# Two-layer graph network on one core: where VectorE's addition to the logits of four groups stands in the first edge pass

## The reference, cut to what matters

```python
msg_s = (s_n @ Ws_src)[src] + (s_n @ Ws_dst)[dst]          # and the same for the vectors
m1_s, m1_v = _cg_tp(msg_s, msg_v, y0, y1, w1[...])         # products with the harmonics y and weights rbf @ W_rbf
a = (m1_s @ W_alpha).reshape(e, H, AS_)
a = jnp.where(a > 0, a, 0.2 * a)
a = jnp.sum(a * alpha_dot, axis=-1, keepdims=True)         # the logits: 4 heads for each edge
val_s = m1_s @ Ws_val
val_v = jnp.einsum('ecx,cd->edx', m1_v, Wv_val) * jax.nn.sigmoid(val_s @ Wg)[..., None]
m2_s, m2_v = _cg_tp(jax.nn.sigmoid(val_s), val_v, y0, y1, w2_ss, ...)
h = ...                                                    # m2 @ Ws_vlin and Wv_vlin, weighted by softmax(a) later
```

## Time and profile before

| what | value |
|---|---|
| time, median of 3 runs | 9161.6 us (9114.4 to 9190.4) |
| profiled execution: device time | 9135.8 us |
| profiled execution: span of the instructions | 9134.0 us |
| TensorE busy | 7569 us (83%) |
| VectorE busy | 6767 us (74%) |
| ScalarE busy | 5161 us (57%) |
| mean granted TensorE clock | 0.86 |
| VectorE's additions to the logits | 98, 22.2 us busy, 254.2 us idle before them |

### The profile page before, as it was taken

One profiled execution on the slowest core, in us unless ns is written; L12 is line 12 of the kernel. 1 busy time (PEld: TensorE's weight loads), 2 busy tenths in 40 slices (PEclk: granted clock), 3 DMA queues, 4 the chain that ended last, 5 costly groups with the idle time before them and its releaser, 6 DMA issues. The chain is left out here.

```text
span 9134.0 us, 197714 instructions
## 1 busy us (share of the span) xinstructions
PE 7569.2 (83%) x43972; PEld 5972.6 (65%) x43973; DVE 6766.6 (74%) x16742; ACT 5161.1 (57%) x16950; POOL 5109.3 (56%) x5222
## 2 busy tenths in 40 slices
PE   5788888888888888888888886997778888888788
PEld 3677777777777777777777776995444444444446
DVE  7777777777777777777777787887667767767677
ACT  5555555555555555555555552116666666667675
POOL 0556666555555555655655555870666655566650
PEclk7788888888788788888888797998899989999999
DMA  7333333223222232322332234766444434444345
GB/s 251 79 83 87 85 85 84 79 83 85 79 83 83 79 85 83 84 83 81 84 83 83 82 80 150 236 204 112 107 110 111 112 106 110 111 109 114 108 110 180
DMA packets 971877, 968.06 MB, mean 106 GB/s; under 512 B 452750, under 2 KB 788750, under 8 KB 971662
## 3 DMA queue, kind: packets, MB, share of 16 engines
q0 software_dynamic: 225792, 385.65, 17.1%
q1 hardware_dynamic: 512032, 346.40, 13.8%
q10 hardware_dynamic: 233936, 234.90, 7.7%
HBM read 677.57 MB, written 288.65 MB: 106 GB/s over the span
## 5 line engine op out<-in xcount | busy, mean ns | idle before, releaser
L754 POOL DMA_INDIRECT e_g_dst<-table_dst,e_idx x1568 | 1518.9, 969 | 1159.5 <-issue 622.8
L754 POOL DMA_INDIRECT e_g_src<-table_src,e_idx x1568 | 1560.9, 995 | 996.6 <-issue 803.3
L2028 POOL DMA_INDIRECT f_e<-table,f_src x1568 | 1494.0, 953 | 980.1 <-issue 530.3
L793 PE MATMUL e_ps_t<-ident,e_m 128*128 128x128 f32 (+1 forms) x7840 | 1405.9, 331 | 471.1 <-issue 193.2
L793 PEld LDWEIGHTS e_ps_t<-ident,e_m 128*128 128x128 f32 (+1 forms) x7840 | 1121.6, 168 | 618.4 <-issue 365.8
L2085 PE MATMUL f_ps_a<-sums 128*128 128x384 f32 x3936 | 1524.3, 534 | 1.5 <-DVE sums L2185 1.5
L2085 PEld LDWEIGHTS f_ps_a<-sums 128*128 128x128 f32 x3936 | 767.6, 205 | 576.0 <-issue 228.7
L886 ACT ACTIVATE e_m1t<-e_ps_t 128x512 f32<-128x512 f32 (+1 forms) x1176 | 669.1, 597 | 548.9 <-PE e_ps_t L809 198.1
L2074 PE MATMUL f_ps_w<-f_w,f_hidden 64*128 64x192 f32 x3936 | 495.1, 374 | 470.3 <-DVE sums L2185 232.3
L1013 DVE TENSOR_TENSOR e_vy<-e_msg,e_ps_w 128x384 f32<-128x384 f32 x392 | 216.5, 552 | 839.5 <-issue 522.1
L905 ACT ACTIVATE e_ps_v<-e_ps_v 128x128 f32<-128x128 f32 x392 | 102.7, 262 | 1252.7 <-remote 733.3
(11 more groups left out here) (268 smaller groups left out, 17539.2 us busy)
## 6 DMA issues: line engine op xcount, KB each, us to landing
edge_values<-e_h ACTq DMA_DIRECT2D x392, 330.0 KB
r_h<-edge_values SPq DMA_DIRECT2D x196, 660.0 KB, 4.0
sums<-sums ACTq DMA_DIRECT2D x492, 192.0 KB
e_g_src<-table_src,e_idx POOLq DMA_INDIRECT x1568
e_g_dst<-table_dst,e_idx POOLq DMA_INDIRECT x1568
f_e<-table,f_src POOLq DMA_INDIRECT x1568
f_rbf<-basis SPq DMA_DIRECT2D x492, 48.0 KB
basis<-t_part SPq DMA_DIRECT2D x42, 448.0 KB, 3.1
```

Of the source, the lines that this page charges most:

```text
L754: pool.indirect_dma_start(out=into[:, r, t, :], out_offset=None, in_=table, in_offset=bass.IndirectOffsetOnAxis(ap=idx[:, r, c:c + 1], axi ...
L793: last = nc.tensor.transpose(ps_t[bank][0:channels, t * P:(t + 1) * P], rows(t), ident[:])
L2028: pool.indirect_dma_start(out=rows_of_units[:, (place * RING + r) * T + t, :], out_offset=None, in_=table, in_offset=bass.IndirectOffsetOn ...
```

## The change

The call of `leaky` for the same four groups moves within VectorE's program: from the end of the body of r = 1 to the body of r = 2, behind `products_with_y`. The argument names the same groups as before (u is larger by one, so one more is taken off). Its wait, its instruction and its semaphore stay. The call after the last round, for the last four groups, is unchanged, so 97 of the 98 additions move. No other engine's program changes.

```diff
@@ body of VectorE, edges @@
                 message_of_tile(r, 3)
                 gated_with_y(w)
                 products_with_y(u)
+                if r == 2:
+                    leaky(u - RING - 2)
                 second_dot_of_two(w)
                 dot_of_two(u)
                 second_cross_of_two(w)
@@
                 heads_sum(x, rx, nx)
                 vectors_by_weights(u)
                 cross_by_weights(u)
-                if r == 1:
-                    leaky(u - RING - 1)
 
             rounds(dve, body)
```

## The result

The changed kernel takes 9209.9 us (median of 16 executions, 9163.2 to 9282.4); the kernel before takes 9158.5 us (16 executions, 9114.4 to 9206.3). The ratio is 1.0064, with a 95% interval of 1.0043 to 1.0085. The forecast was 9150 us in a range of 9095 to 9195: the time lies outside the range and on the other side of no change, though within the 1% that the prediction took for no change. The profiled execution took 9201.8 us (span 9200.0) against 9135.8 us (9134.0). That pair differs by 66 us, the ratio gives 59 us. (The ratio is not the quotient of the two medians, which is 1.0056.)

A forecast was written before the change was run, and what follows sets the result against it. The loop was taken as bound by TensorE at low clock, VectorE at full. Gains of 34 + 5 us less 21 us net 18 us; two thirds, 12 us, off 9161.6 gave about 9150 us, range 9095 to 9195.

The forecast's parts named there:

- Part 1: VectorE before the additions: the 2.59 us waits disappear, but only 34 us of some 251 us are gained.
- The 34 us of lateness: VectorE's own delay in starting the third group's products with y after `with_y0`, 0.35 us a round, counted as gain.
- Part 2: TensorE's `mix`, held up by VectorE's late restart: 5 us gained, bounds 0 and 11.8 us.
- Part 3: The addition in VectorE's third group delays what follows by 0.22 us a round; cost 21 us if VectorE leads.
- the 21 us: Cost of the moved addition on VectorE, 97 x 0.22 us, if VectorE leads the loop.
- Part 4: ScalarE's `keep` waits for the later addition; by the order of the programs this costs nothing.
- The round: Four groups of the first edge pass, expected to be shorter by some 0.1 us.
- The whole stall on the path: Rival: all of VectorE's waiting before the additions goes, 251 us, giving 8911 us; chance 0.03.
- the rising clock: Rival: fewer gaps on TensorE raise its clock by 0.02, giving 9096 us; chance 0.22.
- Only the 0.22 us are left: Rival: VectorE's won time vanishes into TensorE's work, the addition lengthens the third group, 21 us more: 9183 us; chance 0.18.
- Slower, by the clock: Rival: the 0.22 us delay opens gaps on TensorE, its clock falls by 0.02, giving 9204 us; chance 0.07.

The follow-up runs named there:

- e12_wait_all_moved: Kernel before with the wait for ScalarE's copies in every group and the addition behind the third group's products with y; 9059.8 us, ratio 0.9933.
- e3_wait_all: Kernel before with the wait for ScalarE's copies at the end of every group's VectorE body, not only r = 1; 9499.4 us, ratio 0.9923.
- e1_ahead: Changed kernel with the addition one place further up, ahead of the third group's products with y, still without the wait; 9626.4 us, ratio 1.0063.
- e2_wait: Changed kernel with the wait alone put back at its old place, the addition staying behind the products with y; 9590.6 us, ratio 1.0026.
- e4_wait_1_3: Kernel before with a second wait for ScalarE's copies, at the end of the body of r = 3; 9541.5 us, ratio 0.9970.
- e13_sbuf: Kernel before plus two VectorE products at each group's end, all operands from SBUF, and a wait for `gated`; 9433.4 us, ratio 0.9971.
- e14_psum: Kernel before plus two VectorE products at each group's end, one operand from PSUM, and a wait for `gated`; 9491.2 us, ratio 1.0008.
- e5_work: Kernel before plus two VectorE products on SBUF operands at each group's end, 1.9 us of work, no more waits for ScalarE's copies; 9037.2 us, ratio 0.9951.

## Why the prediction was wrong, point by point

**Part 1, the wait is removed: the events right, the worth wrong.** The idle time before the additions fell to 0.0 (under 10 us expected), and went to the products with y (1124.9 us, about 1000 expected) and to `mixed_with_y` (155.1, about 165 expected). The step that failed is the reading of the earlier trace rows: the 11.60 us group against the 10.79 us group was booked as 0.81 us that the wait costs. The short group didn't show what a group is like without a wait: it was short only with the addition at its old place behind the wait, and in the other arrangements it had about 12 us or more (the table at e12_wait_all_moved). The group with the wait, at 12.04 us, was no longer than the 11.81 and 12.37 us of groups without one. The 34 us of lateness did go (6 us are left), but the step from there to the time failed: counted from the group before, the third group's `with_y0` came 0.71 us later (13.41 against 12.70 us), twice the 0.35 us won, and the third group itself then takes 1.18 us more in the mean of the rounds. Where a gain of 34 us stood in the sum, groups at full clock lost 53 us and the rarer full clock 37 us in the profiled pair. Behind this stands an assumption of the whole sum: that work which starts earlier can't end later. No term allowed for a loss there, and e3_wait_all shows that the waits are worth having (0.9923).

**Part 2, the mix: wrong sign, small.** Its idle time rose from 24.8 to 34.9 us, where 5 us were to be gained. The share put down to e_d did fall, from 11.8 to 5.2 us; the other shares grew by more.

**Part 3, the moved instruction: the 21 us neither shown nor excluded.** e12_wait_all_moved against e3_wait_all differs by 0.1%, less than the two can tell, and e1_ahead, without the instruction in that place, loses as much as the change. In the third group at full clock the place shows, and by more than 0.22 us: 12.08 us in e2_wait against 10.95 us in e4_wait_1_3, both behind a wait and on one chip. The idle time of the heads went from 257.3 to 248.4 us; for those that wait for the third body's `heads_sum` it went from 0.64 to 0.59 us each, so the 0.2 us more that were forecast aren't there.

**Part 4, ScalarE: right.** In the groups by line of the changed kernel, what ended the waits before `above` is TensorE's heads most of all, and never VectorE's addition:

```profile
L926 ACT ACTIVATE e_above<-e_ps_h 128x16 f32<-128x16 f32 x392 | 72.2, 184 | 318.0 <-PE e_ps_h L838 255.7 <-remote 42.1 <-issue 19.4
```

**The round** was to be shorter by 0.1 us; it went from 53.67 to 54.65 us. The pass is longer by 92 us, which the prediction named only with the other sign as what would make it wrong.

**The rivals.** The whole stall on the path (8911 us) and the rising clock (9096 us) fall. "Only the 0.22 us are left" (9183 us) came nearer than the forecast, but its cause can be a part of the loss at most, since e1_ahead has the loss without that delay. "Slower, by the clock" (9204 us) came nearest: 37 of the 92 us are groups that lost the full clock. But its mechanism, the delay of the moved instruction, has against it e12_wait_all_moved, which has that delay and a clock 0.006 higher than before, and e1_ahead, which doesn't have it and has a clock 0.005 lower. The clock of the pass fell by 0.011 (0.831 to 0.820 over the 376 groups), not by 0.02, and the 37 us that go with it are 34 us for 0.01, where the prediction had 27 us from two stretches of one trace. The premise of that rival, that a group's clock follows from gaps on TensorE, has a poor row in the changed kernel too: TensorE is busy for 14.13 of 14.13 us in the group from 4512.90 and was granted 0.61 there. The Trainium skill, TensorE: Matmul & The Clock Gate (Part 1), has the gate opened by recent work of the array; that row doesn't agree with it by itself.

**What stays open.** By which mechanism an early second product hurts. Shown are: waits in all groups are worth 1.3% against none, and the lost wait is the main cause of the loss; a late start works whether VectorE idles or does SBUF work in its place; it isn't the bytes of the gathers; the first message may go early; and the operand's memory of work on VectorE in that stretch changes the time and the clock. That it isn't the time of the mix is likely, not shown; what share the place of the addition has is open. That the second product's reads of PSUM, earlier and beside the heads, cost the full clock in the same way would fit, but no run moved those reads alone, and the gathers' longer issues with SBUF operands are the rival to it for that pair. It wouldn't explain the full groups' 0.58 us. The lengths of ScalarE's instructions give no hint (`with_y0` took 319 ns each in e13_sbuf and in e14_psum), and the records can't settle it for TensorE, since a matmul's end is modelled in them.

## What to carry to other kernels

A wait on an engine that has slack may be a useful brake, as here: before removing it, compare the groups behind it with the others at the same clock, and try the opposite change as well, a wait in every turn of the loop; here that gave the best version (0.9923, against 1.0064 for the removal). A group that is short beside one with a wait doesn't show what the wait costs; the wait may be why it is short. In a sum of such a change, let "starts earlier" have both signs. Where one engine's clock is granted and not given, read how many turns of the loop had the full clock, and how long these were, apart from each other.

## What the hardware did that I had not expected

- 1.9 us more work on VectorE in every group, on SBUF operands, made the kernel faster by 0.5% (e5_work). With one operand from PSUM, and one more wait, that was gone (1.0020); with the same wait in both it was 1.0008 against 0.9971 on another chip, with a clock lower by 0.006. GpSimd's issue of a gather of target rows took 1034 ns beside the products on SBUF and 964 ns beside those with the PSUM operand.
- Gathers of a twentieth of the bytes made the kernel slower by 3.3%, with a clock of 0.78 in the pass where full ones had 0.83 in the profiled kernel before.
- Chips differ by more than any change here: the kernel before took from 9093.9 to 9567.8 us (medians), with mean clocks of 0.867 and 0.840.
